# Cross attention: the adding up of a head's five weighted samples moves from VectorE to GpSimd

## The reference, cut to what matters

```
sk = 0.5 * (w0 * _gather_pad0(Kh, i0) + w1 * _gather_pad0(Kh, i1))
sv = 0.5 * (w0 * _gather_pad0(Vh, i0) + w1 * _gather_pad0(Vh, i1))
scores = jnp.einsum('bhqd,bhqkd->bhqk', Qh / math.sqrt(HD), sk)
attn = jax.nn.softmax(scores, axis=-1)
ctx = jnp.einsum('bhqk,bhqkd->bhqd', attn, sv)
```

## Time and profile before

| what | us |
|---|---|
| median of 3 runs | 2389.03 (2388.89 to 2389.97) |
| the profiled execution, its own time | 2390.54 |
| its span | 2388.8 |
| PE busy | 1900.7 (80%) |
| DVE busy | 1553.9 (65%) |
| POOL busy | 1153.7 (48%) |
| ACT busy | 921.8 (39%) |
| cross attention, first product (L1421) to last normalisation (L1302) | 1586 to 2220 of the span |

### The profile page before, as it was taken

How to read it: one execution, slowest core, us unless ns; L and a number is a source line. 1 busy time by engine, 2 the same in 40 slices (tenths; PEclk the granted TensorE clock), 3 DMA queues, 4 the chain that set the end, 5 groups by cost and what they waited for, 6 DMA issues and landing times. The chain is left out here.

```text
span 2388.8 us, 41441 instructions
## 1 busy us (share of the span) xinstructions
PE 1900.7 (80%) x16815; PEld 1114.6 (47%) x16815; DVE 1553.9 (65%) x2578; ACT 921.8 (39%) x1279; POOL 1153.7 (48%) x934
## 2 busy tenths in 40 slices
PE   6888878888878888888888889568787787785476
PEld 3444444444444444444444444345565555664232
DVE  6675656666656656767657553156868868775676
ACT  0222222222222222222222223166775756873376
POOL 0455435445535544654554556216355553555247
PEclk7999989999989999999999999789999999997686
DMA  7122123112222211211121120200000000000102
GB/s 214 29 62 45 41 51 74 36 39 65 45 56 50 60 39 44 61 43 41 44 64 41 34 58 23 70 2 7 2 2 7 2 2 2 2 2 1 41 1 71
DMA packets 57263, 93.98 MB, mean 39 GB/s; under 512 B 26608, under 2 KB 39024, under 8 KB 52592
## 3 DMA queue, kind: packets, MB, share of 16 engines
q1 hardware_dynamic: 47856, 91.06, 15.3%
q10 hardware_dynamic: 9216, 0.27, 0.2%
HBM read 53.02 MB, written 4.46 MB: 24 GB/s over the span
## 5 line engine op out<-in xcount | busy, mean ns | idle before, releaser
L779 POOL TENSOR_TENSOR acc<-acc,probs 128x1024 f32<-128x1024 f32 (+3 forms) x320 | 553.0, 1728 | 145.0 <-ACT probs L517 116.2
L517 ACT ACTIVATE probs<-psum 128x1024 f32<-128x1024 f32 (+3 forms) x384 | 290.3, 808 | 645.0 <-PE psum L423 645.0
L415 PE MATMUL psum<-operands 64*128 64x512 f32 (+3 forms) x1536 | 315.7, 517 | 59.8 <-DVE turned L586 23.5
L638 DVE TENSOR_REDUCE maxes<-psum 128x2 f32<-128x1024 f32 (+1 forms) x224 | 268.4, 1223 | 132.0 <-PE psum L393 121.8
L1214 ACT ACTIVATE onehot<-psum 128x1024 bf16<-128x1024 f32 x320 | 322.1, 1035 | 3.0 <-PE psum L1054 3.0
L1073 PEld LDWEIGHTS psum<-piece,onehot 128*128 128x128 bf16 x7680 | 264.1, 100 | 100.9 <-ACT vs L1221 33.2
L439 PE MATMUL psum<-probs,vals 128*64 128x512 f32 (+3 forms) x1536 | 295.6, 507 | 4.4 <-POOL probs L760 4.4
L1073 PE MATMUL psum<-piece,onehot 128*128 128x64 bf16 x7680 | 274.7, 195 | 30.4 <-ACT vs L1221 24.9
L1593 POOL TENSOR_TENSOR vs<-vs,wgt 128x1280 f32<-128x1280 f32 x64 | 154.9, 2421 | 282.7 <-DVE wgt L1461 282.7
L760 POOL TENSOR_SCALAR_AFFINE_SELECT probs<-probs 128x256 f32<-128x256 f32 x256 | 131.7, 526 | 285.1 <-ACT probs L517 285.1
L1054 PE MATMUL psum<-i0T,near 128*128 128x512 bf16 x640 | 199.5, 396 | 83.4 <-ACT onehot L1214 76.5
(11 more groups left out here) (215 smaller groups left out, 3140.5 us busy)
## 6 DMA issues: line engine op xcount, KB each, us to landing
operands<-turned SPq DMA_DIRECT2D x124, 256.0 KB, 4.3
rden<-inverse_rows SPq DMA_DIRECT2D x64, 256.0 KB, 3.8
wqk<-in_wqk SPq DMA_DIRECT2D x16, 512.0 KB, 3.2
wv<-in_wv SPq DMA_DIRECT2D x16, 256.0 KB, 2.6
y<-in_x SPq DMA_DIRECT2D x1, 4096.0 KB, 19.5
wo<-in_wo SPq DMA_DIRECT2D x16, 256.0 KB, 2.6
out<-res SPq DMA_DIRECT2D x16, 256.0 KB, 2.1
xT<-in_xT SPq DMA_DIRECT2D x3, 1024.0 KB, 6.7
```

Of the source, the lines that this page charges most:

```text
L415: nc.tensor.matmul(dst[:, hh, 0:width], ops[n % 2][rows, 1, kt * P:(kt + 1) * P].bitcast(F32), ops[n % 2][rows, 0, a:a + width].bitcast(F3 ...
L517: nc.scalar.activation(probs[u % PBUF][:, :, 0:width], slot("s", n, u)[:, :, 0:width], ACT.Exp, scale=1.0 / D ** 0.5).then_inc(s_exp, 1)
L638: V.reduce_max(maxes[:, :, place_of[0]:place_of[-1] + 1:step], src[:, :, 0:len(parts) * width].rearrange("p h (k q) -> p h k q", q=width), ...
L779: G.tensor_tensor(dst, dst, src, ALU.add).then_inc(s_acc, 1)
```

## The change

For all rounds but the last, POOL adds a head's five samples itself, right behind its weighing, in three additions: samples 2 and 3 onto 0 and 1 (256 elements a partition), then 1 onto 0 (128), then 4 with 0 into `ctx2` (128). Each waits for the one before. DVE's 60 calls of `gather` in the rounds go; the four of the last round stay, and the last of them now waits until `s_c2` has its 15 counts from POOL. The wait for `s_c2t` goes to POOL as well.

```
--- before.py
+++ after.py
-GATHER_AT = [(2, 1), (2, 3), (3, 1), (3, 3)]
...
+        s_part = sem("samples_added_in_part")
...
-                if h == 0 and b:
-                    dve.wait_ge(s_c2t, KT * b)
                 dve.wait_ge(s_wv, HG * r + j + 1)
...
                 if j == HG - 1:
+                    dve.wait_ge(s_c2, r)
                     ins.then_inc(s_c2, 1)
...
-                    if r and (j, u) in GATHER_AT:
-                        gather(r - 1, GATHER_AT.index((j, u)))
...
+            def sum_samples(r, j):
+
+                b, hg = divmod(r, NHG)
+                h = hg * HG + j
+                n = HG * r + j
+                pool.wait_ge(s_wv, n + 1)
+                v = vs[:, r % 2, j, :, :].rearrange("p t (k c d) -> p t k c d", k=NK, c=2)[:, :, :, 0, :]
+                G.tensor_tensor(v[:, :, 0:2, :], v[:, :, 0:2, :], v[:, :, 2:4, :], ALU.add).then_inc(s_part, 1)
+                pool.wait_ge(s_part, 2 * n + 1)
+                G.tensor_tensor(v[:, :, 0, :], v[:, :, 0, :], v[:, :, 1, :], ALU.add).then_inc(s_part, 1)
+                pool.wait_ge(s_part, 2 * n + 2)
+                if h == 0 and b:
+                    pool.wait_ge(s_c2t, KT * b)
+                ins = G.tensor_tensor(ctx2[:, :, h * HD:(h + 1) * HD], v[:, :, 0, :], v[:, :, 4, :], ALU.add)
+                if j == HG - 1:
+                    ins.then_inc(s_c2, 1)
+
...
                     G.tensor_tensor(pair[:, :, 0, :], pair[:, :, 0, :], pair[:, :, 1, :], ALU.add).then_inc(s_wv, 1)
+                    if r < ROUNDS - 1:
+                        sum_samples(r, j)
```

## The result

| | median of 20 runs, us | lowest to highest |
|---|---|---|
| before | 2385.76 | 2379.68 to 2392.74 |
| changed | 2392.83 | 2384.16 to 2403.57 |

The ratio is 1.0033, with a 95% interval of 1.0022 to 1.0043: the change costs about 7.9 us (0.0033 x 2386), between 5.2 and 10.3. The forecast was 9.6 us, so direction and size hold. The forecast's absolute time, 2398.6 us, is 5.8 us above the median of 2392.83; 3.3 of these come from the kernel before, whose median over 20 runs is 2385.76 rather than the 2389.03 of the three runs shown earlier. The profiled execution took 2399.95 us, its span is 2398.2 us, 9.4 more than before.

The account below looks back on a forecast made before the run. No engine was full in the cross attention; a ring of waits bound it. Stalls 11.5, blocking 11.4 + 8.4 + 9.0 + 3.1, less 33.8 of relief, gave +9.6 us: 2398.6 us, range 2383 to 2411.

Parts of the forecast that it names:

- The stalls at softmax: Softmax of rounds 4, 12, 14 and 15 waits for GpSimd's later end of weighing, costing 11.5 us together.
- The price of the sum: GpSimd's three additions take 2.1 us a head, between bounds of 1.6 and 2.65 us.
- the dear rival: GpSimd's additions take 2.65 us a head, making it the bound in more rounds: 2410 us, chance 0.12.
- The relief: Moving sums off VectorE gives back 33.8 us in the rounds where softmax does not wait for the burst.
- The plain rounds: Where nothing else is on VectorE, moving the sums gives 2.4 us a round; 7.2 in rounds 3, 7 and 11.
- ScalarE waits 1.72 us behind a sum, all of it is on the path: Rounds 2, 6 and 10, with sample positions on VectorE, gain 4 x 1.27 = 5.1 us each, 15.3 us.
- The blocking: The longer GpSimd burst holds up VectorE instructions at positions, softmax, bias and normalisations, costing 31.9 us.
- then all do: In round 8's last head all eight normalising instructions meet the burst, two before; softmax 3.1 us later, sums' saving counted.
- Rounds 1 and 2: In round 1 the bias lands on the mask's cast (2.1 us), kv and softmax pay 1.6; moved sums give 1.7.
- hidden by this one: Copies into the values' buffer and the head outputs' transpose come at least 2.3 us behind softmax's start, hidden by its wait.
- both cancel: No change, 2384 to 2393 us, if blocking is 20 rather than 32 us or stalls 5 rather than 11.5; chance 0.21.
- the relief wins: VectorE was the ring's bound and its relief counts: faster, centre 2380 us, once blocking costs under some 17; chance 0.19.

Follow-up runs that it names:

- e2: The changed kernel with sums left out; GpSimd does additions of the same sizes on an unread tile behind each round's four weighings; 2364.56 us, ratio 0.992 to before.
- e1: The changed kernel with the five weighted samples added by nobody in rounds 0 to 14, so the output lacks these sums; 2346.57 us, ratio 0.9843 to before.
- e10: The changed kernel with GpSimd adding only for rounds 1, 2, 5, 6, 9, 10 and 12, sums behind the four weighings; 2360.77 us, ratio 0.9889 to before.
- e8: The changed kernel with the sums of rounds 0, 4 and 8 back on VectorE; 2385.37 us, ratio 1.0008 to before.
- e3: The changed kernel with two tiles for the weights, so softmax waits for the weighing of the round before last; 2380.33 us, ratio 0.9997 to before.
- e7: The changed kernel with a round's four sums behind all four weighings; 2368.42 us, ratio 0.9939 to before.
- e4: The changed kernel with the sums of rounds 3, 11, 13 and 14 back on VectorE; 2375.31 us, ratio 0.9966 to before.
- e6: The changed kernel with GpSimd adding only for rounds 1, 2, 5, 6, 9, 10 and 12; 2365.52 us, ratio 0.9922 to before.

## Why the prediction was right, and where its parts were not

**The stalls at softmax: right.** Place, number and size came out. The forecast had weighing end 22.2 us after the burst's start, it was 21.5; four stalls in rounds 4, 12, 14 and 15, and there were these four. The prediction's 11.5 us in these rounds, and the 9.6 us of relief that it took as lost there (4 x 2.4), are 21.1 us; the changed kernel against e2, which has the load and not the wait, shows 20.9. (Of these e2 pays 2.6 back at the end, +3.7 against +1.1, where its additions stand ahead of the last weighing.)

**The price of the sum: 1.87 us a head, not 2.1.** The small additions of 128 took 0.46 us rather than 0.53, and that of 256 took 0.74, not 0.80. The runs of 16 elements, for which the dear rival stood, showed no price of their own. The Trainium skill (GPSIMD Engine Reference, "Engine selection") has GpSimd about twice as slow for elementwise work with two inputs. For the same operation the trace agrees: 640 elements a partition take GpSimd 1.55 us and VectorE 0.81, a factor of 1.9. The prediction's 2.5 us set this factor on VectorE's reduction, which is another operation; three additions against one reduction are 1.65 us against 1.27, a factor of 1.3.

**The relief: somewhat over-sized.** The prediction had 33.8 us, and 9.6 more lost in the stalls, 43.4 in all; e1 shows 34.0 for the same rounds. The plain rounds held (16.1 us measured in rounds 3, 4, 7, 11, 12, 14, 15, 16.8 forecast; the parts that the prediction names, 0.64 + 0.7 + 0.95, add to 2.3 rather than its 2.4, and 2.3 is what was measured). The gap is in rounds 2, 6 and 10: e1 gains 4.8 us there, against 15.3 forecast from "ScalarE waits 1.72 us behind a sum, all of it is on the path". But these are the intervals that hold the blocked softmaxes of rounds 1, 5 and 9, 8.3 us longer in e1; with them added back the three rounds gain 13.1. So that step was only a little too high. What failed is that the prediction let the relief pass free: coming earlier, VectorE runs into pieces that GpSimd has always had there. For softmax of rounds 5 and 9 this stood at nothing, for round 1 at a part of 1.6 us. In sum over all lines VectorE's instructions are 6.1 us longer in e1 than before (the cast of the mask is 3.7 shorter), so the relief by itself is 34.0 + 6.1 = 40.1 us. This is an estimate: it takes each longer microsecond as one on the path. How the gain splits between a round and its neighbour depends on what stands ahead (the interval of round 6 is 2.0 us shorter in e1 and 4.3 in e10, whose round 5 is 1.0 longer), so single rounds are compared with care.

**The blocking: nearly right in sum, less so in its parts.** 31.9 us were forecast. Added up by their own durations, VectorE's instructions that stayed are 28.6 us longer in the changed kernel than before:

| what is longer | forecast, us | measured, us |
|---|---|---|
| sample positions | 11.4 | 9.0 |
| softmax of rounds 3, 4, 7, 11, 12, 14, 15 | 8.4 | 5.0 |
| scalings of kv, cast of the mask, softmax of rounds 1, 5, 9 | 9.0 | 11.0 |
| the normalisations of round 8 | 3.1 (its sums' saving taken off) | 3.9 |

By the stretches it is the same: 18.6 (e2 against e1), 5.5 more in the changed kernel outside the stalled rounds, 6.1 in e1 already, less round 8's own relief of 2.1, which the forecast had counted in: 28.1. The three terms are 20.9 + 28.1 - 40.1 = 8.9 us, where the forecast had 21.1 + 31.9 - 43.4 = 9.6. Relief and blocking are each off by 3 to 4 us in the sense that cancels, and the parts of the blocking cancel among themselves. That the sum came within 2 us of the measured 7.9 is to this extent luck; the mechanism and its three large terms are not.

**Where the blocking went.** The first four steps of softmax took 0.8 us in rounds 3 and 7 and 1.36 in the stalled ones, where 1.84 - 0.53 more was assumed for each: these additions are shorter than what stood beside softmax in the earlier trace rows. Round 8 was +1.4 rather than +4.3 in its interval. The eight normalisations are blocked as said (in pairs, start and us taken):

```profile
1914.53 3.61 DVE L1302 TENSOR_SCALAR y<-y,mv,rstd 128x256 f32<-128x256 f32 x2
...
1918.46 1.03 DVE L1302 TENSOR_SCALAR y<-y,mv,rstd 128x256 f32<-128x256 f32 x2
...
1920.39 3.58 DVE L1302 TENSOR_SCALAR y<-y,mv,rstd 128x256 f32<-128x256 f32 x2
...
1924.88 0.98 DVE L1302 TENSOR_SCALAR y<-y,mv,rstd 128x256 f32<-128x256 f32 x2
```

but two of the four pairs are hardly blocked, at 1.0 us (0.72 alone); "then all do" was wrong for half of them. Of the sample positions' 9.0 us in three rounds, L1389 and L1390 alone give 3.1 in this round, of the 3.8 forecast for it (2.44 + 2.05 against 0.54 + 0.83 before):

```profile
1847.23 2.44 DVE L1389 TENSOR_SCALAR off<-off,length 128x640 f32<-128x640 f32 x1
1849.71 2.05 DVE L1390 TENSOR_TENSOR dx<-off 128x640 f32<-128x640 f32 x1
```

**Rounds 1 and 2: under-sized.** Here the forecast had the bias land on the mask's cast and kv and softmax pay 1.6 us; what happened around softmax of round 1:

```profile
1641.15 4.57 POOL L1549 TENSOR_TENSOR y<-y,rows 128x2048 f32<-128x2048 f32 x1
...
1643.76 2.02 DVE L1331 CAST xmaskf<-xmask 128x77 f32<-128x77 int32 x1
...
1647.25 3.13 DVE L1443 TENSOR_TENSOR soft<-sc,dx 128x40 f32<-128x40 f32 x4
...
1650.41 3.32 DVE L1447 TENSOR_TENSOR soft<-soft,sc 128x40 f32<-128x40 f32 x4
...
1654.12 0.83 DVE L1450 TENSOR_TENSOR soft<-soft,smax 128x160 f32<-128x160 f32 x1
...
1662.31 0.49 DVE L1421 TENSOR_TENSOR prod<-psum,xq 128x320 f32<-128x320 f32 x1 [6.17 <-PE psum L1073]
```

The cast is there, 2.02 us. But the pieces of keys and values, which follow the bias on GpSimd and were all but over when softmax came before, now stand beside it: eight small steps take 6.45 us, 4.1 more than before (1.83 + 0.53), and the third product then waits 6.17 us for TensorE (3.85 before). e8 measures the whole of rounds 1 and 2 at 6.2 us, net of the relief of round 0's sums; the forecast's steps, 3.7 of blocking less 1.7 of relief, give 2.0. What I failed to do is to follow GpSimd's queue one instruction past the bias. It is the same omission as in the relief above, here made worse by the burst that pushes the pieces back.

**Two waits "hidden by this one".** True in the changed kernel, where the transpose and the values' buffer cost nothing of their own; e3 and e7 show that they come out (2.93 us in e3's round 4, 9.2 us in three rounds of e7) once softmax is let through.

**The rivals.** That both cancel (0.21) or that the relief wins (0.19) each needed less than what the stalls cost. Without them the rival of the relief is right: e4, with the four rounds undone, is 8 us faster than before, and e7, with all 60 sums moved and no stall, 12 to 15.

## What to carry to other kernels

Before work is moved to an engine that has room on average, ask who waits for the end of its burst, and put the moved work behind the instruction that the others wait for: the same 180 additions cost 8 us ahead of that instruction and gained 12 (by the stretch) to 14 (by the medians) behind it. Then move it only where the round has room: 28 sums moved gained 18.6 us, and 26.5 with the sums behind the weighings, 20 of them in the stretch (that the second is better than the first is not shown). And price a relief by what is late next, and by what the relieved engine then runs into, not by the busy time that goes: of 76 us that left VectorE, only 36 came back with nothing in their place, and 8 were lost to blocking by work that had not changed.

## What the runs showed of the hardware that I had not expected

**A chain of small VectorE instructions beside a full GpSimd.** Each of them can stand still for a GpSimd instruction: eight steps of 40 elements, 1.06 us alone, took 6.45 us beside bias and pieces, 5.4 inside a weighing (e3) and 2.2 to 2.5 beside the short additions. In these rows the harm goes by the length of GpSimd's instructions: e3 and e7 have the same GpSimd instructions (1254.6 and 1254.7 us busy), and softmax of round 4 takes 5.4 us in one and 2.5 in the other. It also goes by when VectorE comes: e1 has no more load than before and loses 8.3 us in three softmaxes. Here the Trainium skill (SBUF — State Buffer, "Who interferes with whom") has the rule that two engines shut each other out where VectorE has two inputs in SBUF or runs in a two-port mode; the trace agrees, as the product (L1421, one input from PSUM) took 0.49 us in the rows beside GpSimd too. GpSimd pays as well: in the changed kernel its five longest additions of 256 elements took 1.19 to 1.21 us rather than 0.74, and all five ran beside instructions of the sample positions with two inputs.

**TensorE's clock after a stall.** The stretches between these times in the changed kernel, columns as above:

```profile
1755.00:1764.00 9.00, 5.52 (x105) 3.97 (x100) 3.90 (x14) 4.67 (x7) 8.02 (x9) 1.00 0.01 2
1764.00:1766.40 2.40, 0.66 (x5) 0.69 (x6) 1.83 (x5) 1.24 (x3) 0.00 (x0) 0.92 0.00 0
1766.40:1769.80 3.40, 3.40 (x46) 2.93 (x46) 0.71 (x2) 2.57 (x5) 0.00 (x0) 0.56 0.00 0
```

Behind the stall of round 4, with TensorE busy for 0.66 of 2.4 us, the granted clock was 0.56 for 3.4 us: the lower of its two levels (1.2 GHz) for most of them. The same came behind the stalls of rounds 12 and 14, with 0.57 over 2086 to 2092 and 0.51 over 2155 to 2160 us, where the kernel before has 1.00 in all of these stretches. Over the measured stretch the changed kernel spent 67 us at the lower level and the one before 42; e1 27, e6 24, e10 40 and e4 47. More of it goes with the stalls, but e4 is faster than the kernel before with more, so this time orders nothing by itself; what it adds to a stall's price was not separated.

**Spread.** Executions of the changed kernel lie between 2384 and 2404 us. Part of the spread is outside the cross attention, whose first product came between 1572.0 and 1586.1 us in the twelve profiled executions, though no edit but a short memset in e1 and e2 touches what is ahead of it. The cause stays open.
